# A routed mixture-of-experts layer behind a recurrent attention: out-projection and ranks by tiles of 128 tokens

## The chip, the cores and the metric

The kernel runs on one core of a Trainium2 chip. The metric is the device time of one execution in microseconds (us), a median over several executions. Five engines work side by side, each through its own queue of instructions: TensorE (PE) multiplies and writes to PSUM, its weight loads are listed apart as PEld; VectorE (DVE), ScalarE (ACT) and GpSimd (POOL) do the elementwise work; SyncE (SP) starts transfers. They wait for each other by semaphores (`wait_ge`, `then_inc`).

## What is computed

1088 tokens (16 images or texts with 68 positions each), width 256, everything in float32. The reference, cut to what matters:

```python
h = concat(patches(x) @ W.T + b, (weight_l @ weight_r)[x_txt])        # embed: 36 + 32 tokens each
h = h + attn(layernorm(h))                                             # 16 heads of 64, gated recurrence
h = h + ffn(layernorm(h))                                              # 8 experts, the best 2 of each token
# attn: S_t = a_t * S_(t-1) + k_t v_t^T;  o_t = q_t S_t;  out @ W_o
# ffn:
probs = softmax(xn @ Wg);  top_vals, top_idx = top_k(probs, 2);  top_vals /= sum(top_vals)
out   = sum over the two experts e of top_vals * (relu(xn @ W1[e] + b1[e]) @ W2[e] + b2[e])
```

## The kernel before

It has four stages, each written by hand for every engine, in the order in which the instructions stand in each queue; nothing reorders them.

**Attention** goes by pairs of heads (`HP` = 8 pairs), tokens along the free axis. A pair's scores (L549) and mixes with the values (L565) go by four groups of 272 tokens (`GT`), 12 and 16 matmul instructions each in the trace; between a group's scores and its mix stands the causal mask on DVE (L1168, `mask`). ACT copies each mix into `oT` (L936). Within the pairs 1 to 7 the groups of the pair before stand between the projections of the next pair. The last pair has no next pair beside it: L631 to L635 order its groups as scores 0, scores 1, mix 0, scores 2, mix 1, scores 3, mix 2, mix 3, with two pairs of PSUM banks for the scores. Before it a one-element matmul (L630) and `ok_sum` decide whether a general path is needed (it is not, with these inputs); `s_way` says so to every engine.

**Out-projection, norm, routing.** `out_projection(g, m)` (L672) puts the features on partitions: per group of 272 tokens and half `m` of the width, 8 matmuls with `wo` as weights. DVE adds the result to the stream `hT` (L1263). Mean and variance are matmuls with a matrix of 1/256 (L682, L689), the square and the root are ACT's (L1045, L1049), centring and normalising DVE's (L1269, L1275, L1278). `logits` (L699) has the experts on partitions; ACT copies it (L1053), and `turn_logits` (L749) turns it to tokens on partitions. `turn_stream` (L741) and `turn_rows` (L732) turn the stream and the normalised rows, ACT copies them to `hrow` (L1023) and `xrow` (L1016), SP writes `xrow` to memory (L396, L398).

Only then, for all nine row tiles at once, DVE does the softmax, the two best experts (`top`, `topi`), `pick` (one-hot, 9 tiles x 2 picks x 8 experts) and `share`. Two matmuls (L827 with a strict triangle `tri`, L829 with `mean_w`) count the picks before each token; DVE works out from them the rank of each pick in its expert's blocks of 128 rows (L1334 to L1354), then `in_block` (L1355) and `at_place` (L1359); POOL makes `entry` (L1546). 18 matmuls (L837) turn these into the table of the 24 blocks; DVE takes the row numbers `gather_u` and `scatter_u` out of it. PE runs `keep_warm` in the waits: 7 multiplications of 512 columns before the table, 5 behind it (L484, two instructions each in the trace).

**Experts.** 24 blocks of 128 rows: POOL gathers the rows (L1552), PE turns them (L760), `up` (L777 to L779), `turn_h` (L788), `down` (L798); DVE and ACT copy between; POOL scatters (L1559). w1 is split by POOL into `w1hi` and `w1lo` beforehand (L1537, L1539), once the attention is done and its last quarter has been loaded (L389, L1535).

**Combine.** SP loads both rows of each token, DVE adds them with `share` to `hrow` (L1429, L1433), SP stores.

## Time and profile before

| | us |
|---|---|
| median of 3 runs | 389.0 |
| lowest and highest of them | 388.13, 389.59 |
| the profiled execution, its own time | 388.07 |
| its span, first to last instruction | 386.3 |
| around the span | 1.8 |
| mean granted TensorE clock, as a share of full speed | 0.958 |

The times below are us from the start of the span. The stage of experts begins at 273.4 and its matmuls end at 366.9; the scatter, the loads and the combine take the rest. PE is busy 90% of the span. A float32 matmul shows as two instructions in the trace, one of type float32r as one; a transpose as one.

### The profile page before, as it was taken

To read this page: it belongs to the slowest core of one execution; us is meant where nothing else is said; L and a number is where in the kernel's file an instruction comes from. 1 tells how busy PE (TensorE), PEld (TensorE's weight loads), DVE (VectorE), ACT (ScalarE), POOL (GpSimd) and SP (SyncE) were. 2 spreads that over 40 slices of the span, in tenths; PEclk is the share of its full clock that TensorE was granted. 3 is DMA by queue.
4 is the path that set the end of the run, shared out by engine and by line. 5 is a ranking of instruction groups with operands and counts; after the bars stand their busy time and mean duration, and the time that the engine had idled before them with its cause. 6 is when DMAs were issued, how large, how long until landed. Compare 5 with 4: busy or idle time off the path is not lost.

```text
span 386.3 us, 7120 instructions
## 1 busy us (share of the span) xinstructions
PE 348.6 (90%) x2545; PEld 297.7 (77%) x2546; DVE 219.0 (57%) x333; ACT 115.2 (30%) x255; POOL 139.3 (36%) x147
## 2 busy tenths in 40 slices
PE   4989999999999999999799999698799999999900
PEld 3664999999999999999787886474588888888800
DVE  1056898758586857796930354585344545454326
ACT  1035453353435252523211111530123233232300
POOL 5632025231224113131233995005435555463310
PEclk9999999999999999999989999887999999999965
DMA  7920006022020200000009600030111221222156
GB/s 216 291 86 0 2 5 216 1 88 93 3 97 0 97 2 2 2 2 0 3 2 372 283 0 0 2 116 14 54 42 68 70 75 67 74 71 55 42 171 216
DMA packets 12093, 28.95 MB, mean 75 GB/s; under 512 B 2144, under 2 KB 6752, under 8 KB 11552
## 3 DMA queue, kind: packets, MB, share of 16 engines
q1 hardware_dynamic: 9632, 21.99, 16.0%
q0 software_dynamic: 2432, 6.56, 5.8%
q8 instruction: 20, 0.33, 0.4%
q14 instruction: 9, 0.07, 0.1%
HBM read 23.17 MB, written 5.37 MB: 74 GB/s over the span
## 4 chain that ended last, share of the span: by engine, by line
PE 66%; issue 9%; POOL 8%; DVE 7%; DMA 6%; SPq 1%; ACT 1%; POOLq 0%; DVEq 0%
PE ps L798 10%; PE ps L428 7%; PE ps L549 7%; PE ps L565 6%; PE ps L429 6%; PE ps L430 6%; POOL w1lo L1539 5%; PE ps L777 3%; PE ps L779 3%; PE ps L778 3%; PE ps L525 3%; PE ps L788 3%; DMA pt<-patches 2%; POOL w1hi L1537 2%; PE ps L526 2%
## 5 line engine op out<-in xcount | busy, mean ns | idle before, releaser
L428 PE MATMUL ps<-xnhi,wlo 128*128 128x272 f32 x192 | 57.9, 301 | 0.9 <-DVE xnlo L1136 0.9
L1161 DVE RECIPROCAL invU<-U 128x272 f32<-128x272 f32 x32 | 57.6, 1827 | 0.0
L429 PE MATMUL ps<-xnlo,whi 128*128 128x272 f32 x192 | 55.4, 288 | 0.0
L430 PE MATMUL ps<-xnhi,whi 128*128 128x272 f32 x192 | 55.3, 288 | 0.0
L1037 ACT ACTIVATE hr<-ps,b 128x128 f32<-128x128 f32 x96 | 27.4, 369 | 80.3 <-PE ps L788 80.3
L1486 POOL TENSOR_TENSOR qA<-qraw,invU 128x544 f32<-128x544 f32 x16 | 22.4, 1398 | 71.8 <-DVE invU L1161 34.9
L798 PE MATMUL ps<-w,hr 128*128 x192 | 45.2, 379 | 0.0
L1559 POOL DMA_INDIRECT yrows<-yb,scatter_u x24 | 24.5, 1020 | 40.4 <-DVE yb L1401 36.9
L428 PEld LDWEIGHTS ps<-xnhi,wlo 128*128 128x128 f32 x192 | 36.1, 188 | 2.8 <-issue 1.7
L798 PEld LDWEIGHTS ps<-w,hr 128*128 128x128 f32 x192 | 34.7, 190 | 3.8
L1168 DVE TENSOR_TENSOR pb<-ps,causal 128x592 uint32<-128x592 uint32 (+3 forms) x32 | 27.5, 858 | 17.4 <-PE ps L549 17.1
L429 PEld LDWEIGHTS ps<-xnlo,whi 128*128 128x128 f32 x192 | 36.2, 189 | 0.0
L430 PEld LDWEIGHTS ps<-xnhi,whi 128*128 128x128 f32 x192 | 36.1, 188 | 0.0
L1475 POOL TENSOR_TENSOR wlo<-wraw,whi 128x768 fp32r<-128x768 f32 x8 | 17.5, 2182 | 42.0 <-ACT bneg L897 42.0
L549 PE MATMUL ps<-qA,kU 64*128 64x136 f32 (+8 forms) x384 | 30.8, 294 | 0.7 <-issue 0.7
L565 PE MATMUL ps<-pb,vt 128*64 128x136 f32 (+8 forms) x512 | 29.2, 255 | 2.4 <-DVE pb L1168 2.1
L672 PE MATMUL ps<-oT,wo 128*128 128x272 f32 x128 | 30.5, 394 | 0.7 <-ACT oT L936 0.7
L565 PEld LDWEIGHTS ps<-pb,vt 128*64 128x64 f32 x512 | 25.4, 139 | 7.1 <-DVE pb L1168 3.3
L1552 POOL DMA_INDIRECT xg<-xrows,gather_u x24 | 24.9, 1037 | 14.9 <-issue 6.4
L1143 DVE TENSOR_TENSOR_SCAN U<-u_g,first 128x544 f32<-128x544 f32 x16 | 21.0, 1310 | 16.2 <-ACT u_g L918 16.2
L549 PEld LDWEIGHTS ps<-qA,kU 64*128 64x128 f32 x384 | 27.2, 193 | 3.1 <-issue 0.9
L672 PEld LDWEIGHTS ps<-oT,wo 128*128 128x128 f32 x128 | 24.2, 190 | 6.1 <-issue 1.2
(176 smaller groups left out, 608.2 us busy)
## 6 DMA issues: line engine op xcount, KB each, us to landing
w<-w SPq DMA_DIRECT2D x1, 4096.0 KB, 14.7
wraw<-w_attn SPq DMA_DIRECT2D x8, 384.5 KB, 3.6
w<-w SPq DMA_DIRECT2D x6, 512.0 KB, 4.2
yin<-yrows SPq DMA_DIRECT2D x4, 384.0 KB, 4.7
wv<-w_v SPq DMA_DIRECT2D x4, 256.0 KB, 2.7
wo<-w_o SPq DMA_DIRECT2D x1, 1024.0 KB, 13.4
w<-w SPq DMA_DIRECT2D x1, 1024.0 KB, 5.2
b<-b SPq DMA_DIRECT2D x1, 1024.0 KB, 16.7
```

The lines of the kernel that those rows point to most:

```text
L428: pe.matmul(dst, slo, mhi[n], start=(i == 0), stop=False)
L429: pe.matmul(dst, shi, mlo[n], start=False, stop=False)
L430: last = pe.matmul(dst, shi, mhi[n], start=False, stop=(i == len(pairs) - 1))
L549: last = pe.matmul(ps[:, bank + h, at:at + t1 - t0], kU[par][k, r * P:(r + 1) * P], qA[par][k, t0:t1], start=True, stop=True)
L565: last = pe.matmul(ps[DK * h:DK * (h + 1), bank, lo - GT * g:hi - GT * g], vt[(a // 2) % 2][:, r, par * P + DK * h:par * P + DK * (h + 1)] ...
L672: last = pe.matmul(ps[:, 2 * (g % 2) + m, 0:GT], wo[:, a, m * P:(m + 1) * P], oT[:, a, g * GT:(g + 1) * GT], start=(a == 0), stop=(a == HP ...
L798: last = pe.matmul(ps[:, 5 + par, 0:D], hr[par][:, j * P:(j + 1) * P], w2[:, bass.ds(e, 1), j * D:(j + 1) * D].rearrange("p o n -> p (o n) ...
L1037: last = act.activation(hr[par][:, j * P:(j + 1) * P], ps[:, 3 + par, j * P:(j + 1) * P], ACT.Relu, bias=col)
L1161: dve.reciprocal(invU[:, g * GT:(g + 1) * GT], U[:, g * GT:(g + 1) * GT]).then_inc(s_a, 1)
L1168: dve.tensor_tensor(pb[g % 2][:, :, 0:PW[g]].bitcast(U32), ps[:, bank:bank + 2, 0:PW[g]].bitcast(U32), keep, ALU.bitwise_and).then_inc(s_p, 1)
L1552: pool.indirect_dma_start(out=xg[b % XG][:], out_offset=None, in_=xrows, in_offset=bass.IndirectOffsetOnAxis(ap=gather_u[:, b:b + 1], axis=0),
L1559: pool.indirect_dma_start(out=yrows, out_offset=bass.IndirectOffsetOnAxis(ap=scatter_u[:, b:b + 1], axis=0), in_=yb[b % NY][:], in_offset= ...
```

## The change

The scores of the last pair keep one pair of banks (4 and 5) like those of the other pairs, and its groups run as scores 0, mix 0, scores 1, mix 1, and so on. The out-projection behind them goes by nine tiles of 128 tokens (the last one overlaps the one before by 64), tokens on partitions, with `oT` as weights and `wo` streaming; the stream is added on PE, by two matmuls of `hT` with the identity. ACT copies each tile to `hrow`. DVE takes mean and variance with `bn_stats` and `bn_aggr`, normalises into `xrow`; PE turns each tile (`turn`), ACT copies it (`xT`), PE multiplies it with `wg` (tokens on partitions at once), DVE chooses the two best by `max` and `max_index` of the logits (`choose`), and PE adds each tile's picks into the ranks of all later picks (`count`, in float32r). All of that stands between the tiles of the out-projection. The softmax is taken of the eight sorted logits, behind the table (`low`, `weigh` after the third block). `entry` is made by DVE, pick by pick, beside `at_place`. SP writes each normalised tile twice, once per pick, so `gather_u` comes straight out of the table. POOL's split of w1 no longer waits for the last quarter of w1.

```diff
@@ PE
-                if early(a, HP) and a == HP - 1 and g:
-                    pe.wait_ge(s_p, 4 * a + g - 1)
-                    pe.wait_ge(s_o, 4 * a)
-                    pe.wait_ge(s_vev, VC * IT)
-                elif not (early(a, 1) and g == 0):
+                if not (early(a, 1) and g == 0):
                     pe.wait_ge(s_p, 4 * a + g)
...
-            for g in range(G):
-                pair_scores(HP - 1, 1, g, bank=4 + 2 * (g % 2))
-                if g:
-                    mix(HP - 1, 1, g - 1, bank=3 - (g - 1) % 2)
-            mix(HP - 1, 1, G - 1, bank=3 - (G - 1) % 2)
+            def out_part(r, a0, a1):
+                tok, bank = slice(token0(r), token0(r) + P), OPB[r % len(OPB)]
+                if a0 == 0:
+                    if r >= len(OPB):
+                        pe.wait_ge(s_hrow, r - len(OPB) + 1)
+                    for m in range(DC):
+                        pe.matmul(ps[:, bank, m * P:(m + 1) * P], hT[:, m, tok], ident[:], start=(m == 0), stop=False)
+                for a in range(a0, a1):
+                    last = pe.matmul(ps[:, bank, 0:D], oT[:, a, tok], wo[:, a, :], start=False, stop=(a == HP - 1))
+                if a1 == HP:
+                    last.then_inc(s_op, 1)
+            pair_scores(HP - 1, 1, 0)
+            mix(HP - 1, 1, 0, bank=6)
+            pair_scores(HP - 1, 1, 1)
+            mix(HP - 1, 1, 1, bank=7)
...
+            for r in range(4):
+                out_part(r, 0, HP)
+            out_part(4, 0, half_a)
+            turn(0)
+            out_part(4, half_a, HP)
+            turn(1)
+            out_part(5, 0, half_a)
+            logits(0)
...
+            out_part(8, half_a, HP)
+            logits(5)
+            turn(6)
+            count(5)
+            turn(7)
+            logits(6)
+            pe.wait_ge(s_hrow, 6)
+            keep_warm(1, 0)
+            turn(8)
+            count(6)
+            logits(7)
+            logits(8)
+            count(7)
+            count(8)
...
-            keep_warm(7, 3)
+            keep_warm(3, 0)
             for a in range(A):
-                if a % RT == 0:
-                    pe.wait_ge(s_place, a // RT + 1)
-                    pe.wait_ge(s_entry, a // RT + 1)
+                pe.wait_ge(s_place, a + 1)
@@ DVE
+            def take_moments(r):
+                dve.wait_ge(s_hrow, r + 1)
+                link(dve.bn_stats(spread[r % 2][:], hrow[:, r]))
+                dve.bn_aggr(moments[:, r], spread[r % 2][:]).then_inc(s_mom, 1)
+            def choose(r):
+                dve.wait_ge(s_lgmm, r + 1)
+                logits = ps[:, 6, r * E:(r + 1) * E]
+                link(dve.max(top[:, r, :], logits))
+                link(dve.max_index(topi[:, r, :], top[:, r, :], logits))
+                dve.tensor_tensor(pick[:, r], expert_no[:, r],
...
+            for r in (7, 8):
+                take_moments(r)
+                choose(r - 3)
+                normalise_of(r)
+            for r in range(6, RT):
+                choose(r)
...
-            for i in range(PICKS):
-                a = slice(i * RT, (i + 1) * RT)
-                dve.tensor_tensor(at_place[:, a], place[:].unsqueeze(1).to_broadcast([P, RT, P]),
-                                  place_of[:, a].unsqueeze(2).to_broadcast([P, RT, P]), ALU.is_equal
+            for a in range(A):
+                dve.tensor_scalar(entry[:, a, :], block_start[:], border[:, a:a + 1],
+                                  row_no[:, a // PICKS, a % PICKS:a % PICKS + 1], ALU.is_equal, ALU.mult)
+                dve.tensor_scalar(at_place[:, a, :], place[:], place_of[:, a:a + 1], None, ALU.is_equal
                                   ).then_inc(s_place, 1)
@@ POOL
-            pool.wait_ge(s_w1, 16 * EARLY_W + 16)
+            pool.wait_ge(s_w1, 16 * EARLY_W)
             for e in range(E):
+                if e == EARLY_W:
+                    pool.wait_ge(s_w1late, 16)
```

PE's order at the start of the last pair. Before, L549 (scores) of groups 0 and 1, then L565 (mix) of group 0; `pb` is the masked score tile:

```order
L549 MATMUL ps<-qA_100,kU_98 128x136 x2
L549 MATMUL ps<-qA_100,kU_98 128x144 x2
L549 MATMUL ps<-qA_100,kU_98 128x16 x2
L549 MATMUL ps<-qA_100,kU_98 128x136 x2
L549 MATMUL ps<-qA_100,kU_98 128x160 x2
L549 MATMUL ps<-qA_100,kU_98 128x32 x2
L565 MATMUL ps<-pb_103,vt_102 64x136 x2
```

After (L535 is the scores' line there, L551 the mix's):

```order
L535 MATMUL ps<-qA_101,kU_99 128x136 x2
L535 MATMUL ps<-qA_101,kU_99 128x144 x2
L535 MATMUL ps<-qA_101,kU_99 128x16 x2
L551 MATMUL ps<-pb_104,vt_103 64x136 x2
L551 MATMUL ps<-pb_104,vt_103 64x8 x2
L551 MATMUL ps<-pb_104,vt_103 64x136 x2
L551 MATMUL ps<-pb_104,vt_103 64x16 x2
L535 MATMUL ps<-qA_101,kU_99 128x136 x2
```

The scores of group 1 have moved behind the mix of group 0, and so with the later groups.

PE's order from the end of the out-projection to the table, before (L732, L741: rows turned; L827, L829: counts; L484: `keep_warm`; L837: table):

```order
L741 MATMUL ps<-ident,hT 128x128 x8
L732 MATMUL ps<-ident,xc 128x128 x8
L732 MATMUL ps<-ident,xc 32x128 x2
L732 MATMUL ps<-ident,xc 128x128 x8
L732 MATMUL ps<-ident,xc 32x128 x2
L827 MATMUL ps<-pick,tri 128x144
L829 MATMUL ps<-pick,mean_w 128x144
L484 MATMUL ps<-first,mean_w 128x512 x7
L837 MATMUL ps<-entry,at_place 128x24 x18
```

After, from the last half tile of the out-projection (L627) on (L687: logits, L678: `turn`, L697: `count`, L474: `keep_warm`, L817: table):

```order
L627 MATMUL ps<-wo,oT 128x256 x4
L687 MATMUL ps<-wg,xT_127 128x8 x2
L678 MATMUL ps<-ident,xrow 128x128 x2
L697 MATMUL ps<-pick,ones_m 128x64
...
L678 MATMUL ps<-ident,xrow 128x128 x2
L687 MATMUL ps<-wg,xT_126 128x8 x2
L474 MATMUL ps<-first,mean_w 128x512
...
L697 MATMUL ps<-pick,tri 128x16
L474 MATMUL ps<-first,mean_w 128x512 x3
L817 MATMUL ps<-entry,at_place 128x24 x18
```

The long turns and the two counts of all tiles are gone from here; small pieces of the last tiles have taken their place.

## Rows read from the trace of the kernel before

**Rows 1.** Engines by stretch: length, busy (count) PE, PEld, DVE, ACT, POOL, clock, DMA, GB/s.

```profile
203.33:241.47 38.14, 38.14 (x164) 29.99 (x164) 13.24 (x17) 5.34 (x10) 27.58 (x16) 1.00 0.40 166
241.47:256.15 14.68, 11.70 (x65) 9.21 (x65) 9.12 (x43) 7.67 (x14) 0.00 (x0) 0.77 0.01 2
256.15:266.39 10.24, 8.88 (x33) 5.16 (x32) 8.56 (x22) 0.79 (x2) 3.22 (x2) 0.93 0.33 109
273.36:366.00 92.64, 90.69 (x478) 77.66 (x477) 44.60 (x95) 27.44 (x96) 44.29 (x43) 1.00 0.19 61
```

**Rows 2.** Waits from 200 to 290: who <- for whom: us in total, times, longest.

```profile
POOL entry L1546 <- DVE in_block L1355: 24.4, 1, 24.4
POOL w1hi L1537 <- DMA w<-w: 12.4, 1, 12.4
```

**Rows 3.** Timeline of the last pair: start, duration, engine, line, count [idle before <-releaser].

```profile
193.10 1.44 PE L565 MATMUL ps<-pb,vt 128*64 128x136 f32 x16 [1.85 <-DVE pb L1168]
194.59 2.64 PE L549 MATMUL ps<-qA,kU 64*128 64x136 f32 x24
196.18 0.78 DVE L1168 TENSOR_TENSOR pb<-ps,causal 128x592 uint32<-128x592 uint32 x1 [1.34 <-PE ps L549]
...
199.66 0.99 PE L549 MATMUL ps<-qA,kU 64*128 64x136 f32 x12
...
200.70 0.97 DVE L1168 TENSOR_TENSOR pb<-ps,causal 128x784 uint32<-128x784 uint32 x1 [0.83 <-PE ps L549]
...
201.73 0.92 PE L565 MATMUL ps<-pb,vt 128*64 128x136 f32 x16 [0.24 <-DVE pb L1168]
...
203.33 11.24 PE L672 MATMUL ps<-oT,wo 128*128 128x272 f32 x48 [0.68 <-ACT oT L936]
```

**Rows 4.** PE alone by stretch: length, busy (count), granted clock, DMA, GB/s.

```profile
191.00:192.00 1.00, 0.24 (x6) 1.00 0.00 0
192.00:193.00 1.00, 0.00 (x0) 1.00 0.00 0
...
194.00:195.00 1.00, 1.00 (x14) 0.50 0.00 0
...
197.00:198.00 1.00, 1.00 (x24) 1.00 0.00 0
```

**Rows 5.** Back-to-back small PE work; the first is from the chain, the rest timeline.

```profile
281.96 1.73 PE ps L798 x8
...
241.47 1.07 PEld L741 LDWEIGHTS ps<-ident,hT 128*128 128x128 f32 x10 [0.46 <-issue]
...
249.03 1.03 PEld L749 LDWEIGHTS ps<-ident,lgT 8*128 8x128 f32 x9 [1.29 <-issue]
...
262.96 1.08 PEld L837 LDWEIGHTS ps<-entry,at_place 128*128 128x128 f32 x9 [1.67 <-DVE at_place L1359]
```

**Rows 6.** DVE and ACT pieces: timeline rows, and lines by source (ns min/median/max).

```profile
251.87 0.71 DVE L1312 MAX8 top<-pr 128x8 f32<-128x8 f32 x9
256.15 0.31 DVE L1334 TENSOR_SCALAR total<-ps 128x144 f32<-128x144 f32 x1 [0.95 <-PE ps L829]
260.35 0.18 DVE L1354 TENSOR_TENSOR border<-pos,place_of 128x18 f32<-128x18 f32 x1
375.06 1.28 DVE L1429 SCALAR_TENSOR_TENSOR yin<-yin,share,hrow 128x256 f32<-128x256 f32 x3 [7.67 <-DMA yin<-yrows]
...
L1195 DVE TENSOR_SCALAR causal<-causal x1: 872/872/872, 45.8 to 45.8; 128x1376 int32<-128x1376 f32 x1
L1366 DVE TENSOR_SCALAR owner_i<-owner x1: 178/178/178, 265.1 to 265.1; 128x24 int32<-128x24 f32 x1
L1026 ACT ACTIVATE hrow<-ps x1: 377/377/377, 243.7 to 243.7; 128x256 f32<-128x256 f32 x1
```

**Rows 7.** Timeline of PE at the table and behind it.

```profile
264.62 1.73 PE L837 MATMUL ps<-entry,at_place 128*128 128x24 f32 x9 [0.48 <-POOL entry L1546]
266.20 7.32 PE L484 MATMUL ps<-first,mean_w 128*128 128x512 f32 x10
```

More of the change, by code:

```diff
@@ L744, in turn_logits @@
-            def turn_logits():
-                pe.wait_ge(s_lgt, G)
-                for r in range(RT):
-                    t0 = min(r * P, TOK - P)
-                    last = pe.transpose(ps[:, 4, r * E:(r + 1) * E], lgT[:, t0:t0 + P], ident[0:E, 0:E])
-                last.then_inc(s_lgtok, 1)
+            turn(3)
+            out_part(6, 0, half_a)
+            logits(2)
+            count(0)
+            out_part(6, half_a, HP)
+            logits(3)
+            count(1)
+            turn(4)
@@ new lines, in _ @@
+            out_part(7, 0, half_a)
+            count(2)
+            out_part(7, half_a, HP)
+            count(3)
+            logits(4)
+            turn(5)
+            out_part(8, 0, half_a)
+            count(4)
+            out_part(8, half_a, HP)
[10 more added lines that the diff above has]
+            logits(8)
@@ L1071, in _ @@
-            stream_rows(1, 5, RT)
-            rows(2, 0, 6, 3)
-            rows(3, 1, 0, 2)
+            act.activation(pr[:], low[:], ACT.Exp).then_inc(s_exps, 1)
             act.wait_ge(s_owner, 1)
@@ new lines, in _ @@
+            normalise_of(4)
+            choose(0)
+            take_moments(5)
+            choose(1)
+            normalise_of(5)
+            choose(2)
+            take_moments(6)
+            choose(3)
+            normalise_of(6)
+            for r in (7, 8):
[4 more added lines that the diff above has]
+                choose(r)
+            rank = ps[:, 7, 0:A * E].rearrange("p (a e) -> p a e", e=E)
@@ L1418, in _ @@
                 block_step(b, b % 2)
+                if b == 2:
+                    weigh()
             copy_h(NB - 1, 1)
```

428 lines of the change are left out of this document (164 added, 264 removed).

## The prediction

> **What bounds the kernel now.** I read the engines by stretch first, then the timeline around the last pair, then the waits. Up to 203 the kernel is attention and barely touched. From 203.33, the first matmul of the out-projection, to 241.47 PE has no gap [rows 1]: that stretch is PE's own work. From 241.47 to 256.15 PE is busy 11.70 of 14.68 us at a mean clock of 0.77, because norm, logits, softmax and choice hand over to each other. From 256.15 to 266.39 DVE is busy 8.56 of 10.24 us: it works out ranks and table while PE fills the time with `keep_warm`. Then the ten `keep_warm` instructions behind the table run, 7.32 us to the end of the last [rows 7], and the experts start at 273.36. Their stretch has PE busy 90.69 of 92.64 us and is not touched, nor is what follows. So the time of the change is the time from 194.59, the first scores of the last pair [rows 3], to 273.36: 78.8 us, of which 8.7 lie before 203.33 and 70.0 behind it.
>
> POOL looks prominent in the chain of waits with its split of w1, but it then waits 24.4 us for DVE's `in_block` [rows 2]. Taking the last quarter of w1 out of its first wait, part of the 12.4 us there, moves work with over 20 us of cover. I count nothing. The cover stays, since the table comes no earlier than some 60 us after the attention's end. Writing the normalised rows twice is covered too: 18 transfers, issued between PE's tiles, the last about 10 us before the gather that needs it; SP has nothing else to do there.
>
> **The last pair: a loss, and the largest term.** Before, PE has the next group's scores to do while DVE masks. After, it has nothing: scores g+1 stand behind mix g, and mix g waits for mask g. At full clock a group's scores take about 0.95 us (0.99 with the end of the last) and a mix 0.80 (0.92 with its end) [rows 3]. The four masks grow from 0.78 to 0.97 us, together 3.5. With 0.2 us per group for handing over (scores end to mask about 0.05, mask end 201.67 to mix 201.73 and up to 0.15 elsewhere) and the 0.68 us to the first out-projection, the pair takes 4 x 1.75 + 3.5 + 0.8 + 0.7 = 12.0 us against 8.74: 3.3 more.
>
> That holds at full clock. The trace shows what gaps do just there: PE is idle from 191.24 to 193.10, and then the clock is at 0.50, 1.2 GHz, through 194 to 196, and back at 2.4 GHz by 197 after PE had worked without a gap [rows 4]. At the low level the mix of 16 took 1.44 us and the first scores lasted from 194.59 to the mask at 196.18, about 1.5 us [rows 3], so a group costs 1.5 + 1.37 instead of 1.75, 1.12 more. The kernel after enters the pair in the same state, but then works about two thirds of the time with a hole of about 1 us in each group, where before it had none. I expect that not to bring the clock back, or to bring it back and lose it again: three of four groups at the low level, 3.4 more. Term: **+6.7**.
>
> The out-projection then starts at 1.2 GHz. The shortest low stretch in the trace lasts 3.4 us, from 193.3 to 196.6, its inside in [rows 4]; half speed over it loses 1.7 us. Term: **+1.7**.
>
> A rule speaks to this. In the Trainium skill, page "TensorE: Matmul & The Clock Gate", section "Why this matters for your kernels", only idle gaps between bursts that are clearly longer than these are said to throttle the engine. By it the pair would cost the 3.3 us alone, and the sum would be the first rival's below. This case's trace does not bear it out: the clock fell behind a gap of 1.85 us.
>
> **From the first tile to the last: PE work.** Nearest row for a float32 matmul with 256 streaming columns is L798: 8 instructions in 1.73 us, 0.216 each [rows 5]. A tile has 8 of them, 16 instructions: 3.46 us. The addition of `hT` is 4 instructions of 128 columns; the turns of L741 pass at 1.07/10 = 0.107 [rows 5] and I take that, 0.43 a tile. The upper end is the 0.19 that one weight load lasts, if those are not hidden: 3 us more over nine tiles. Nine tiles: 35.0. Between them, up to the last tile's end: six turns (12 x 0.107 = 1.3), five logits (20 instructions; L749 with 8 columns passes at 0.115: 2.3), five counts (16 instructions; L837 with 24 columns passes at 0.12: 1.9). I add 0.9 for some thirty switches between short runs, an estimate at 0.03 each. Together **41.4**, where before 38.1 went to 241.47: 1152 instead of 1088 tokens and the additions on PE cost what mean and variance gave back. DVE and ACT keep up here: per tile of over 4 us DVE has under 2 us.
>
> **From the last tile to the ranks.** Here steps wait for each other. Counted from tile 8's end: the copy on ACT 0.1 + 0.38 (L1026); `bn_stats` of 256 about 0.42 and `bn_aggr` 0.2, with a handover 0.7; `choose(5)`, which DVE has in front of `normalise_of(8)`, three small instructions of 0.18 with two handovers, 0.67; reciprocal and normalisation 0.65. That is 2.5. PE meanwhile does count 5, turn 7, logits 6 and stands at 3.0; `keep_warm(1)`, two instructions of 0.43, delays turn 8 to 3.9. Then turn 8, count 6, logits 7, which `choose(7)` follows, logits 8, `choose(8)`, count 8: 0.25 + 0.36 + 0.5 + 0.65 + 0.5 + 0.7 + 0.4. The ranks stand 7.4 us behind the last tile. Most of PE's pieces here are tiny, so I give 0.4 for the low clock in `keep_warm`, which costs 0.85 if it falls wholly there: **7.8**. Before, from 241.47 to the start of L1334 at 256.15 [rows 6], the same took 14.7. This is where the change gains.
>
> **Ranks to table.** Before, L1334 at 256.15 to the end of L1354 at 260.53, 4.4 us in 15 instructions [rows 6]; ten of them are left, at their durations 2.7, with the wait 2.8: **2.8**. Then `in_block`, `at_place` and POOL's `entry` took 5.8 us up to 266.35, the end of the table [rows 7]. After, DVE does 36 small instructions. Bounds: L1366 lasts 0.178 with 24 elements, but small instructions without a wait between them start closer together, nine MAX8 in 0.71 us, 0.08 each. `at_place` has 128 elements; `tensor_scalar` did 1376 in 0.87 us, so 128 are about 0.23. Operands per partition cost more: L1429 lasts 0.48 where 256 elements without one last 0.43, and three of them take 1.28, so 0.08 of each overlaps [rows 6]. A pair is at least 0.08 + 0.15, at most 0.18 + 0.29 (no overlap, no fast mode). By L1429, the row nearest in form, 0.155 + 0.20 = 0.355: 18 x 0.355 = **6.4**, between 4.1 and 8.5. PE's matmul behind the last: **0.3**. The three `owner` instructions, 1.3 us, now stand in DVE's queue ahead of `gather_u`; the gathers then land about 6.5 us after the table, just inside the `keep_warm` that follows it.
>
> The Trainium skill, page "VectorE: DVE Perf Modes", section "The TRN2 errata — SBUF-src ops pay a fixed extra latency per instruction", speaks against cutting work this small: every instruction pays its fixed latency. With all of it paid, by L1366 and the 0.23 above, a pair is 0.41 and the loop 7.3 instead of 6.4. The MAX8 row shows that part of it overlaps.
>
> **Behind the table.** `keep_warm(5)` is the same; it ran at the low level first, since PE had done little during the table, and so it will again: **7.0** from 266.35 to 273.36. Its ten instructions at full clock would be 4.3, at the low one 8.5.
>
> **Sum.** Behind the last pair: 41.4 + 7.8 + 2.8 + 6.4 + 0.3 + 7.0 = 65.7 against 70.0, so -4.3. With +6.7 and +1.7: **+4.1**. `weigh`, 1.4 us on DVE after the third block, lies beside PE's work in a stage where DVE is busy 44.60 of 92.64 us: nothing, at worst 1. The profiled execution would be 388.1 + 4.1 = 392.2. It lay 0.9 below the median of the runs; on the median 389.0 the same difference gives 393.1, which I forecast.
>
> **Rivals.**
> *The clock holds in the last pair* (or comes back after the first scores as before). For it: from 197 on the clock was full before, with gaps of 0.24 and 0.68 us at the pair's end [rows 3]. Against: a hole in every group. Then +3.3, +0.6 for the first scores at the low level, no half-speed start, -4.3: 388.6. Chance 0.26.
> *The tail is shorter than I think, with the clock held.* The decision lies in the loop: at 0.23 a pair it is 4.1 us instead of 6.4, and with `keep_warm` ending at the full level 1 us more is won. Then about 385.5. It beats the loss in the last pair from the point at which everything from the first tile to the experts takes under 64 us. Chance 0.16.
> *Everything low.* All four groups at 1.2 GHz (+1.1), a second low stretch at the out-projection (+1.7), slow loads for the additions (up to +3): 397. Chance 0.10.
> *The routing isn't hidden*: PE stalls between tiles for `choose` or the copies, several tenths in each, as each logits waits for the choice before. DVE has 2 us of slack per tile, so small: within the forecast's width.
>
> **How the numbers follow.** Forecast 0.48, 390.5 to 395.5. Range for 8 in 10: from 386.0, which cuts off most of the second rival, to 396.5. A change within 0.5% (1.9 us) cannot be told from none in this kernel. Slower by more: forecast and third rival, 0.56. Within: the first rival and the forecast's lower edge, 0.27. Faster by more: 0.17.
>
> **What would show it.** In the trace after: PE's groups in the last pair at 2.7 us each (clock held) or 3.9 (low), and the clock in the first microseconds of the out-projection; 41.4 us from first to last tile; 7.8 from there to the first rank instruction; the spacing of the 36 small instructions. The forecast is wrong above all if the clock is at 1.00 through the last pair, or if the steps behind the last tile take much more or less than 8 us.

## The result, and the profile after

The changed kernel took 393.58 us (median of 4 runs, 392.58 to 395.94), the kernel before beside it 388.56 us (388.01 to 389.59): a ratio of 1.0145, with a 95% interval of 1.0094 to 1.0196. It is slower. Medians in this document are over all runs, while the ratios and their intervals leave out a run that lies over 1.5% above the fastest of its kernel (none here; in the series below four of f1, two of e3 and one of the kernel before in each). The forecast was 393.1, on the same side and inside its range; three of its steps came out about 1 us too low each, which smaller ones and luck partly made up for.

The profiled execution took 393.43 us, 5.4 more than the one of before (388.07), so the sum of the prediction (+4.1) can be laid beside it term by term. First the engines by stretch in the kernel after. The columns are those of [rows 1]: window and length, busy time (count) of PE, PEld, DVE, ACT and POOL, granted clock, DMA share, GB/s.

```profile
194.35:210.93 16.58, 12.03 (x114) 11.10 (x113) 3.64 (x5) 1.99 (x5) 2.35 (x17) 0.54 0.01 2
210.93:216.04 5.11, 5.11 (x14) 4.30 (x15) 0.00 (x0) 1.49 (x2) 4.94 (x4) 0.50 0.83 309
210.93:254.61 43.68, 43.25 (x231) 38.54 (x231) 17.90 (x52) 8.43 (x24) 26.81 (x16) 0.94 0.50 193
254.61:262.51 7.90, 5.86 (x37) 4.94 (x37) 3.36 (x21) 3.31 (x7) 0.00 (x0) 0.87 0.07 17
262.51:265.12 2.61, 2.61 (x4) 1.06 (x5) 2.26 (x11) 0.00 (x0) 0.00 (x0) 0.50 0.00 0
265.12:272.37 7.25, 6.39 (x21) 4.00 (x19) 7.25 (x37) 0.00 (x0) 0.00 (x0) 0.74 0.00 0
272.37:279.43 7.06, 7.05 (x13) 3.12 (x13) 1.67 (x10) 0.26 (x1) 3.13 (x3) 0.64 0.19 56
```

The windows are, in this order: the last pair; the first 5.11 us of the out-projection, which are part of the next window; all nine tiles; from the last tile to the first instruction of the ranks; the ranks; VectorE's loop over 18 columns; and from there to the first turn of gathered rows. The last pair took 8.74 us before and takes 16.58. From its end to the first turn the kernel before took 70.0 us [rows 1, 3] and this one takes 68.5. So the out-projection and ranks did become shorter, by 1.5 us, and the pair became longer by 7.8. In the loop's window DVE is busy for all of it.

The timeline of PE in the pair (start, duration, engine, line, operation, names, shape, count, and in brackets the idle time before it and what ended that) answers to [rows 3]. L535 are the scores, L551 the mix, L625 the first instruction of the out-projection:

```profile
193.39 0.92 PE L551 MATMUL ps<-pb,vt 128*64 128x136 f32 x16 [1.85 <-DVE pb L1140]
...
194.35 0.88 PE L535 MATMUL ps<-qA,kU 64*128 64x136 f32 x12
196.11 1.52 PE L551 MATMUL ps<-pb,vt 128*64 128x136 f32 x16 [0.88 <-DVE pb L1140]
197.56 1.63 PE L535 MATMUL ps<-qA,kU 64*128 64x136 f32 x12
...
208.69 1.60 PE L551 MATMUL ps<-pb,vt 128*64 128x136 f32 x16 [1.08 <-DVE pb L1140]
210.93 1.19 PE L625 MATMUL ps<-ident,hT 128*128 128x128 f32 x4 [0.65 <-ACT oT L916]
```

Each mix waits 0.88 to 1.08 us for DVE's mask. Before, the next scores hid this wait, except for 0.24 us at the last mix. And everything from the first mix on takes almost twice its time: 1.52 where the first mix of a pair could be 0.88, 1.63 where the scores could be 0.92. The reason is the clock. PE by stretch, with its busy time (count), the granted clock, DMA share and GB/s:

```profile
191.00:194.00 3.00, 1.15 (x22) 1.00 0.00 0
194.00:195.00 1.00, 1.00 (x22) 1.00 0.00 0
195.00:196.00 1.00, 0.23 (x6) 0.78 0.00 0
196.00:197.00 1.00, 0.89 (x10) 0.50 0.00 0
...
215.00:216.00 1.00, 1.00 (x4) 0.50 0.91 385
216.00:217.00 1.00, 1.00 (x6) 0.98 1.14 492
```

The clock falls from 2.4 to 1.2 GHz within the microsecond that starts at 195, is 0.50 through the rest of the pair, and comes back just after 216. Before, it fell earlier, at 193.3, and was back by 197 [rows 4].

### The profile page after: what moved, and what is told of

It is laid out like the page before. It is cut to its first block, busy times and chain, and to the rows that moved or that the text cites. A ratio compares the mean times of both kernels' runs of the same rounds, so it can differ in the third digit from the quotient of the medians.

```text
span 391.7 us, 7260 instructions
## 1 busy us (share of the span) xinstructions
PE 351.2 (90%) x2574; PEld 305.3 (78%) x2575; DVE 220.6 (56%) x381; ACT 113.3 (29%) x263; POOL 135.7 (35%) x145
## 4 chain that ended last, share of the span: by engine, by line
PE 78%; DVE 11%; DMA 4%; issue 3%; SPq 1%; ACT 1%; POOL 0%; POOLq 0%; DVEq 0%
PE ps L803 10%; PE ps L627 8%; PE ps L535 7%; PE ps L551 7%; PE ps L418 7%; PE ps L420 6%; PE ps L419 6%; PE ps L782 3%; PE ps L784 3%; PE ps L783 3%; PE ps L515 3%; PE ps L793 3%; DMA pt<-patches 2%; PE ps L516 2%; PE ps L517 2%
## 5 line engine op out<-in xcount | busy, mean ns | idle before, releaser
L1496 POOL DMA_INDIRECT xg<-xrows,gather_u x24 | 24.9, 1037 | 47.0 <-DVE scatter_u L1310 35.7
L551 PE MATMUL ps<-pb,vt 128*64 128x136 f32 (+8 forms) x512 | 31.3, 267 | 6.0 <-DVE pb L1140 5.8
L551 PEld LDWEIGHTS ps<-pb,vt 128*64 128x64 f32 x512 | 27.4, 147 | 11.0 <-DVE pb L1140 7.4
L627 PE MATMUL ps<-wo,oT 128*128 128x256 f32 x144 | 35.7, 398 | 0.0
L535 PE MATMUL ps<-qA,kU 64*128 64x136 f32 (+8 forms) x384 | 32.2, 302 | 0.7 <-issue 0.7
L535 PEld LDWEIGHTS ps<-qA,kU 64*128 64x128 f32 x384 | 28.4, 199 | 3.2 <-issue 1.3
L627 PEld LDWEIGHTS ps<-wo,oT 128*128 128x128 f32 x144 | 27.9, 201 | 3.6
```

Of the source, the lines that this page charges most:

```text
L535: last = pe.matmul(ps[:, bank + h, at:at + t1 - t0], kU[par][k, r * P:(r + 1) * P], qA[par][k, t0:t1], start=True, stop=True)
L551: last = pe.matmul(ps[DK * h:DK * (h + 1), bank, lo - GT * g:hi - GT * g], vt[(a // 2) % 2][:, r, par * P + DK * h:par * P + DK * (h + 1)] ...
L627: last = pe.matmul(ps[:, bank, 0:D], oT[:, a, tok], wo[:, a, :], start=False, stop=(a == HP - 1))
L1496: pool.indirect_dma_start(out=xg[b % XG][:], out_offset=None, in_=xrows, in_offset=bass.IndirectOffsetOnAxis(ap=gather_u[:, b:b + 1], axis=0),
```

## The experiments

All are compared with the kernel before on the same chip: 387.93 us beside e1 to e4 (median of 25 runs), 388.15 beside f1 to f4 (23), 388.13 beside g1 to g4 (11). The three series ran on three chips, and the result apart from them; where kernels of two series are compared, keep in mind that the kernels before beside them differ by up to 0.6 us. Runs of one kernel spread by 2 to 10 us, mostly with the mean clock of the run, so I go by the traces for where time went, and by medians only where they differ by more than that allows.

| kernel | last pair | us, median (range, runs) | ratio to before [95%] |
|---|---|---|---|
| e1 | old order | 386.31 (384.55–388.45, 10) | 0.9959 [0.9917, 1.0002] |
| e2 (old kernel) | new order | 394.79 (392.11–395.96, 4) | 1.0184 [1.0117, 1.0251] |
| e3 | new order, holes filled | 387.21 (384.12–392.04, 10) | 0.9976 [0.9934, 1.0019] |
| e4 | new order, tiles in the holes | 390.37 (387.68–393.31, 10) | 1.0048 [1.0001, 1.0095] |
| f1 | new order, gap ahead filled | 389.07 (385.36–394.78, 10) | 0.9978 [0.9938, 1.0017] |
| f2 | old order, gap ahead filled | 381.85 (380.62–384.37, 6) | 0.9837 [0.9798, 0.9875] |
| f3 | f2, loop as large instructions | 381.26 (378.58–383.11, 6) | 0.9821 [0.9782, 0.9860] |
| f4 (old kernel) | gap ahead filled | 387.34 (385.49–389.42, 10) | 0.9969 [0.9939, 0.9998] |
| g1 | f2, 3 `keep_warm` for 5 | 382.58 (381.29–383.72, 6) | 0.9846 [0.9795, 0.9897] |
| g2 | f3, 3 `keep_warm` for 5 | 379.46 (376.69–381.08, 6) | 0.9771 [0.9714, 0.9828] |
| g3 | g1, none in the tail | 382.14 (380.04–382.92, 6) | 0.9828 [0.9773, 0.9882] |
| g4 | g2, none in the tail | 379.09 (377.68–379.40, 6) | 0.9754 [0.9703, 0.9804] |

My theory after the result: the last pair's new order costs all of the slowdown, by its holes and by the clock that they keep low, and the new out-projection with its ranks is a gain. Rival: the new out-projection itself is the slower one, and the pair only looks so.

### Half of the change alone: e1 and e2

e1 is the changed kernel with the last pair in the old order:

```diff
-            pair_scores(HP - 1, 1, 0)
-            mix(HP - 1, 1, 0, bank=6)
...
+            for g in range(G):
+                pair_scores(HP - 1, 1, g, bank=4 + 2 * (g % 2))
+                if g:
+                    mix(HP - 1, 1, g - 1, bank=3 - (g - 1) % 2)
+            mix(HP - 1, 1, G - 1, bank=3 - (G - 1) % 2)
```

> The kernel after, with one part undone: the last pair's scores use two pairs of banks again and stand one group ahead of the mixes, as before the change. Theory (the last pair's holes and the low clock that they keep are the whole loss): the pair takes about 8.7 us again instead of 16.6, the out-projection starts at full clock and saves another 2.5, everything behind is as in the kernel after; 393.4 - 7.9 - 2.5 = 383.0, 5 us faster than before the change. Rival (the tiles and ranks cost time themselves): at or above 388.

e2 is the kernel before with only the pair in the new order, the same edit the other way round.

> The kernel before, with only the last pair's groups put in the order scores, mix, scores, mix on one pair of banks. Theory: the pair grows by 7.8 us and the first matmuls of the out-projection run at 1.2 GHz for 3 to 5 us, which costs 1.7 to 2.5; 388.6 + 10 = 398.6. Rival (waits alone, the clock comes back as it did before): plus 3.3 to 3.9, 392.

e1 took 386.31 us, 7.3 below the changed kernel; e2 took 394.79, 6.9 above the kernel before. (The changed kernel was timed apart from them. Each against the kernel before beside it, e1 is at -1.6 and the changed kernel at +5.0, a difference of 6.6.) So the new order costs some 7 us on either kernel, the slowdown is all in it, and the rival is out. Neither size was as expected, though: e1 is 3 us above its forecast, and e2 nearly 4 below its own, between theory and rival. For e1 the timeline of PE and the pair's row by stretch, in the columns of [rows 1], show why:

```profile
193.46 0.92 PE L555 MATMUL ps<-pb,vt 128*64 128x136 f32 x16 [1.83 <-DVE pb L1141]
...
194.43 2.98 PE L539 MATMUL ps<-qA,kU 64*128 64x136 f32 x24
...
203.62 2.06 PE L555 MATMUL ps<-pb,vt 128*64 128x136 f32 x32
206.41 0.68 PE L629 MATMUL ps<-ident,hT 128*128 128x128 f32 x4 [0.72 <-ACT oT L917]
```

```profile
194.43:206.41 11.98, 11.26 (x115) 10.78 (x113) 3.65 (x5) 1.98 (x5) 2.41 (x16) 0.58 0.01 1
```

There is no hole in this pair until its end, and still it takes 12.0 us, at a mean granted clock of 0.58. The 24 scores take 2.98 us, where at full clock they take 1.62 (f2, below). So the clock had fallen behind the gap of 1.83 us ahead of the pair, as in the kernel before, but here it stayed low for some 10 us of work without a pause, where it was back after about 3 in the trace of before. The length of a low stretch is not set by the gap alone, and I had taken the shortest one for the rule.

In e2 the pair grew as expected, but its profiled execution (392.11 us, the lowest of four) got part of it back further on. The first row is the pair, the second the useless products behind the table, which took 7.32 us before [rows 7]:

```profile
194.10:210.03 15.93, 12.02 (x114) 11.09 (x113) 3.64 (x5) 1.59 (x4) 2.06 (x15) 0.55 0.00 1
272.52 4.54 PE L484 MATMUL ps<-first,mean_w 128*128 128x512 f32 x10
```

The pair took 7.2 us more than before, and the out-projection began with 2.7 us at 0.50. The ten useless instructions then ran at full clock, which gave back 2.8 us of the loss. Whether the other three runs, at 394.4 to 396.0, have this too, no trace shows.

### Filling the holes: e3 and e4

e3 puts one useless product of 512 columns into each hole:

```diff
             pair_scores(HP - 1, 1, g)
+            keep_warm(1, 0)
             mix(HP - 1, 1, g, bank=6 + g % 2)
```

> The kernel after, plus one useless product of 512 columns (two instructions, 0.86 us at full clock) between the scores and the mix of each group of the last pair, where PE waits for the mask. It takes no wait away, only the hole. Theory (the clock is what costs most): the clock comes back within the pair as before the change, a group costs about 2.7 us, the out-projection starts at full clock; 386 to 388. Rival (the waits cost, not the clock): 393 or a little more.

It took 387.21 us, as the theory of the clock has it, though three of its ten runs lay at 389.9 to 392.0, with a mean clock of 0.945 to 0.954 for 0.957 to 0.966 in the others. PE in the profiled execution (timeline), and its stretch 194.57 to 206.40 in the columns of [rows 1]:

```profile
193.61 0.92 PE L551 MATMUL ps<-pb,vt 128*64 128x136 f32 x16 [1.85 <-DVE pb L1144]
...
200.84 1.12 PE L474 MATMUL ps<-first,mean_w 128*128 128x512 f32 x2
201.92 0.90 PE L551 MATMUL ps<-pb,vt 128*64 128x136 f32 x16
```

```profile
194.57:206.40 11.83, 11.15 (x123) 7.61 (x121) 3.65 (x5) 1.99 (x5) 2.36 (x17) 1.00 0.01 1
```

With the same gap of 1.85 us ahead of it, the clock is at 1.00 through the whole pair, and the pair takes 11.83 us. That splits the growth of the pair: 11.83 against 8.74 is the part that remains at full clock (3.1 us, the prediction said 3.3), and 16.58 against 11.83 is what the low clock costs in the pair (4.8, the prediction said 3.4). The 8.74 of before holds some low clock itself: at full clock throughout the old order takes 7.90 (f4, below), so the waits of the new order cost 3.9 us and not 3.1. The useless products cost almost nothing there, since DVE's mask takes as long: the groups start 2.7 to 2.8 us apart, where the prediction had 2.7 without them.

e4 puts useful work there, the first seven head pairs of tiles 0 to 3:

```diff
             pair_scores(HP - 1, 1, g)
+            out_part(g, 0, HP - 1)
             mix(HP - 1, 1, g, bank=6 + g % 2)
...
             for r in range(4):
-                out_part(r, 0, HP)
+                out_part(r, HP - 1, HP)
```

> The kernel after, with the first four tiles of the out-projection over the heads of pairs 0 to 6 (18 instructions each, about 3.5 us) between the scores and the mix of each group of the last pair; the rest of each tile behind the pair. The work in the holes is needed anyway. Theory: no holes, full clock, and about 1 us less than with the overlapped order, since no wait for a mask is left: 382. Rival (the mix and its copy now start late and the last one delays the rest): 384 or more.

It took 390.37 us, 3 us more than e3, and my expectation of a gain failed. The clock held in the pair. But what had been moved forward was missing later as a cover. PE's rows with its two longest waits, between the pair and 235:

```profile
224.56 0.41 PE L685 MATMUL ps<-ident,xrow 128*128 128x128 f32 x2 [1.50 <-ACT xT L1026]
231.28 0.58 PE L694 MATMUL ps<-wg,xT 128*128 128x8 f32 x4 [1.79 <-DVE pick L1256]
```

PE stands 1.50 us for the copy of a turned tile and 1.79 for a choice; behind this the clock was at 0.50 from 233.10 to 239.90. This is the last rival of the prediction, the routing that isn't hidden. It was of no weight in the changed kernel, where PE waits once, for 0.43 us, between its first out-projection and 254.61.

DVE is what PE waits for, and DVE is slow here for a reason that the prediction did not have. The same normalisation of 128x256 in e4, twice among the first tiles and once later:

```profile
224.42 2.32 DVE L1249 TENSOR_SCALAR xrow<-hrow,moments,rstd_r 128x256 f32<-128x256 f32 x1
227.86 2.35 DVE L1249 TENSOR_SCALAR xrow<-hrow,moments,rstd_r 128x256 f32<-128x256 f32 x1
243.89 0.41 DVE L1249 TENSOR_SCALAR xrow<-hrow,moments,rstd_r 128x256 f32<-128x256 f32 x1
```

The two long ones lie over POOL's subtractions `w1lo` (224.24 to 226.60 and 227.72 to 230.06) and end 0.14 and 0.15 us after them; from 243.77 on POOL has none and the same instruction takes 0.41. The changed kernel has it too (2.04 us at 222.66, 0.41 from 240.25 on), but with more of PE's work beside it. So in these rows DVE's normalisation ends only when POOL's subtraction has ended. No run without POOL's split was made, so how much of e4's loss that is stays open.

### What brings the clock down: f1, f2, f4

Each of these has two useless products (four instructions) where PE stood idle ahead of the pair:

```diff
+            pe.wait_ge(s_vev, VC * IT)
+            keep_warm(2, 6)
             mix(HP - 2, 0, G - 1)
```

f1 is the changed kernel with them, f2 is e1 with them, f4 the kernel before with them.

> The changed kernel, with two useless products of 512 columns put ahead of the last product of pair 6, so that TensorE works through the 1.85 us in which it stood idle ahead of the last pair. The groups of the last pair are as in the changed kernel, with their holes of some 1 us. Theory A (the idle stretch of 1.85 us brings the clock down, and the holes only keep it there): the clock stays at 1.00 in the last pair, which takes some 12.0 us instead of 16.6, and the time is 386 to 388. Theory B (the holes of some 1 us are enough by themselves to bring the clock down from full): the pair takes 15 to 16.5 us and the time is 392 to 394.

> The changed kernel with the order of the kernel before in the last pair (each group's scores ahead of the mix of the group before it) and the same two useless products ahead of the pair. Without those two, this order took 12.0 us, at 0.50 from just ahead of the pair on. Theory A (the idle stretch ahead of the pair brought the clock down): the clock is at 1.00 through the pair, the pair takes 8.7 us, and the time is some 3 us below the 386.3 of the kernel without the two products, at 383 to 384. Theory B (something within the pair brings it down): as without them, 386 to 387.

> The kernel before, with the two useless products ahead of the last pair, so that TensorE does not stand idle there. Theory A (the clock of the last pair's first scores was already 0.88 to 1.00 in the kernel before, so that nothing is to be had): within 0.5 us of the kernel before. Theory B (the idle stretch sometimes brings the clock down there, and costs some 1 us of the pair): 0.5 to 1.5 us faster.

f2 took 381.85 us, below every run of the kernel before. PE works through the gap, and the pair passes in 7.9 us at full clock. Its timeline and its stretches:

```profile
192.39 1.98 PE L474 MATMUL ps<-first,mean_w 128*128 128x512 f32 x4
194.31 0.92 PE L555 MATMUL ps<-pb,vt 128*64 128x136 f32 x16
...
195.27 1.62 PE L539 MATMUL ps<-qA,kU 64*128 64x136 f32 x24
```

```profile
195.15:203.20 8.05, 6.99 (x118) 6.42 (x115) 3.61 (x5) 1.99 (x5) 2.50 (x17) 1.00 0.01 2
203.20:244.49 41.29, 40.74 (x231) 36.61 (x231) 18.38 (x52) 8.42 (x24) 26.86 (x16) 1.00 0.54 205
244.49:251.94 7.45, 5.11 (x38) 4.19 (x37) 3.36 (x21) 3.31 (x7) 0.00 (x0) 0.98 0.07 18
```

So for the old order theory A holds: the idle stretch ahead of the pair brought the clock down. I had expected 383 to 384; it became 1 to 2 us less, of which 0.8 are explained: the low clock in e1 cost 4.1 us of the pair and not 3.3.

f1 does not decide as neatly. Its profiled execution shows a fall without any idle stretch ahead of the pair:

```profile
191.82 1.98 PE L474 MATMUL ps<-first,mean_w 128*128 128x512 f32 x4
...
196.46 0.88 PE L551 MATMUL ps<-pb,vt 128*64 128x136 f32 x16 [0.88 <-DVE pb L1142]
197.26 0.92 PE L535 MATMUL ps<-qA,kU 64*128 64x136 f32 x12
199.12 1.55 PE L551 MATMUL ps<-pb,vt 128*64 128x136 f32 x16 [0.94 <-DVE pb L1142]
```

```profile
191.87:195.29 3.42, 3.42 (x33) 2.08 (x33) 2.03 (x4) 0.40 (x1) 2.29 (x5) 1.00 0.00 0
195.29:198.70 3.41, 2.01 (x36) 1.77 (x32) 1.25 (x2) 0.40 (x1) 1.68 (x13) 1.00 0.02 5
198.70:209.93 11.23, 8.08 (x73) 7.42 (x73) 2.25 (x3) 1.19 (x3) 0.08 (x1) 0.50 0.01 1
209.93:215.77 5.84, 5.84 (x16) 4.85 (x17) 0.00 (x0) 1.49 (x2) 5.67 (x4) 0.50 0.94 355
```

PE is busy all the time from 191.87 to 195.29, and the clock falls at 198.70. By then PE had had one hole of 0.88 us and stood 0.5 us in the second, which lasted 0.94. So no long gap is needed. But its ten runs do not all look like that. Four took 385.4 to 386.4 us with a mean clock of 0.964 to 0.966, two took 388.5 and 389.7 with 0.953 and 0.954, and four took 392.3 to 394.8 with 0.936 to 0.948; the profiled one is of the last kind. The median of all ten, 389.07, is 0.9 above the kernel before. The first kind has the mean clock of f2 (0.961 to 0.967), and lies near e3. That its clock held through the pair is likely, but only the profiled run has a trace. The changed kernel, with gap and holes, had 0.928 to 0.941 in all four runs. What can be said: the holes of some 1 us in each group can bring the clock down by themselves, and by the mean clocks they do so in some executions and not in others. With the gap in front it was so in all four runs of the changed kernel; four are few to call that a rule.

f4 gained 0.8 us on the kernel before, ratio 0.9969 with an interval from 0.9939 to 0.9998. That is theory B's range, but the interval does not shut out theory A. The traces speak for B: theory A took 0.88 for the clock of the first scores, which is the mean of the whole pair of before, while these scores began at 0.50 [rows 4]. The pair takes 7.90 us in f4, from 194.30 to 202.20, and took 8.74:

```profile
202.20 11.24 PE L674 MATMUL ps<-oT,wo 128*128 128x272 f32 x48 [0.65 <-ACT oT L938]
```

f2 against f4 is the comparison that the change deserves. Both have the old order and a clock of 1.00 in the pair, and they differ by the out-projection, norm and ranks alone: 381.85 against 387.34 us on the same chip, the slowest run of the one below the fastest of the other. Their profiled executions differ by 4.5 (381.89 and 386.37), and their traces place it: the way from the first out-projection to the first turn of gathered rows takes 64.9 us (203.20 to 268.09) against 68.6 (202.20 to 270.78), 3.7 less; the wait for the second part of the combined rows, which varies from run to run (below), is 1.8 shorter in f2; and f2's out-projection starts 1.0 later. So of the 4.5 the traces give 3.7 to the new stages.

### The loop and what hides it: f3, g1 to g4

f3 replaces the 36 instructions of the loop by four:

```diff
-            for a in range(A):
-                dve.tensor_scalar(entry[:, a, :], block_start[:], border[:, a:a + 1], ...
-                dve.tensor_scalar(at_place[:, a, :], place[:], place_of[:, a:a + 1], ...
+            link(dve.tensor_tensor(in_block[:], block_start..., border..., ALU.is_equal))
+            dve.tensor_tensor(entry[:], in_block[:], row_no..., ALU.mult)
+            for i in range(2):
+                a = slice(i * RT, (i + 1) * RT)
+                dve.tensor_tensor(at_place[:, a], place..., place_of..., ALU.is_equal)
```

> The kernel with the old order in the last pair and the two useless products ahead of it, in which also the 36 small instructions of the loop over 18 columns (entry and at_place, 7.25 us in the changed kernel) are 4 large ones: one comparison and one product of 128 x 432 and two comparisons of 128 x 1152. Theory A (VectorE's loop sets when TensorE can form the table, and this sets when the first token rows are turned): the four take some 4 us, the table is there 2 to 3 us sooner after the borders, and the time falls by 1.5 to 2.5 us to some 381. Theory B (the 18 table products on TensorE, or the gather's transfers behind them, set the end): the time stays within 0.5 us.

DVE's timeline: the first pair of the loop's 18 in the changed kernel, and then what f3 has for all 18:

```profile
265.12 0.30 DVE L1296 TENSOR_SCALAR entry<-block_start,border,row_no 128x24 fp32r<-128x24 f32 x1
265.32 0.28 DVE L1298 TENSOR_SCALAR at_place<-place,place_of 128x128 fp32r<-128x128 f32 x1
```

```profile
253.67 0.61 DVE L1299 TENSOR_TENSOR in_block<-block_start,border 128x432 f32<-128x432 f32 x1
254.31 0.61 DVE L1301 TENSOR_TENSOR entry<-in_block,row_no 128x432 fp32r<-128x432 f32 x1
254.83 2.62 DVE L1305 TENSOR_TENSOR at_place<-place,place_of 128x1152 fp32r<-128x1152 f32 x2
```

The small ones start 0.20 us apart, whether they write 24 elements or 128 in a partition: 36 of them are 7.25 us. The large ones take 3.8 for the same result. In the traces f3 is 2.6 us shorter from the borders to the first turn (11.1 for 13.8), but the medians of f3 and f2 differ by 0.6, and their runs overlap. With five products behind the table the point stayed open, so the last four kernels cross two changes, all with three products behind the table instead of five: large or small instructions, and with or without the useless product in the tail, the `keep_warm(1)` that stands between the last tiles' logits and turns.

> The kernel with the old order in the last pair and the two useless products ahead of it, with 3 instead of 5 useless products behind the table (6 instead of 10 instructions). Theory A (these products and not the first gather set when the first token rows are turned; in the trace of the kernel with five the first gather is issued at 263.6, such a transfer takes 1.0 us to issue and 2.9 to land, so that its rows lie there some 1 to 1.7 us before the turn at 268.1): from the end of the table to the first turn some 4.2 us instead of 5.8, and the time 1 to 1.7 us lower. Theory B (the gather sets it, or the clock falls for it and takes the gain back): within 0.5 us of the kernel with five.

> The same with 3 useless products behind the table, and with entry and at_place as four large instructions. Against the kernel with the 36 small ones and the same 3 products: theory A (VectorE's loop sets when the table is there, and all behind it follows): border to first turn 3 us shorter in the trace, the time 2 to 3 us lower. Theory B (the shorter loop moves work against the clock or the gathers, as the medians 381.3 and 381.9 of the two kernels with five products suggest): within 1 us.

> The kernel with the old order, the filled gap ahead of the pair and 3 products behind the table, without the useless product that stands between the last tiles' logits and turns (2 instructions, 1.10 us). Theory A (it stands on the path from the last tile to the ranks, 0.9 us of which the prediction charged to it): last tile to the first instruction of the ranks 6.5 us instead of 7.45, the time 0.5 to 1 us lower. Theory B (TensorE waits at the picks for as long as it saves, or the clock falls earlier and takes it back): within 0.3 us or slower.

> All of it together: old order in the last pair, gap ahead of it filled, 3 products behind the table, four large instructions for entry and at_place, no useless product among the last tiles. If the parts add up (1.5 for the products behind the table, 2 to 3 for the loop, 0.5 to 1 for the tail, from 381.9): 377 to 378. If the clock takes back what the shorter stretches give: 379.5 to 381.

Fewer products behind the table (g1) gained nothing: 382.58 against f2's 381.85 in the series before, so the gain of 1 to 1.7 us that theory A had did not come. Their place was taken by the next thing. PE in g1, and in g2:

```profile
264.52 5.26 PE L474 MATMUL ps<-first,mean_w 128*128 128x512 f32 x6
...
270.29 0.44 PE L768 MATMUL ps<-ident,xg 128*128 128x128 f32 x2 [0.29 <-DMA xg<-xrows,gather_u]
```

```profile
258.58 4.52 PE L475 MATMUL ps<-first,mean_w 128*128 128x512 f32 x6
...
263.97 0.44 PE L769 MATMUL ps<-ident,xg 128*128 128x128 f32 x2 [0.66 <-DMA xg<-xrows,gather_u]
```

Now PE waits for the second gather. In g1 it also stayed at 1.2 GHz for longer: the mean clock from 264.24 to 269.62 is 0.52, where f2 had 0.72 in the corresponding stretch, so its six instructions took 5.26 us for 6.16 that ten took in f2.

The loop, though, counts fully: g2 is 3.1 us below g1 and g4 3.05 below g3, with no overlap of runs in either pair (the nearest are g2's 381.08 and g1's 381.29); from the borders to the first turn g2's trace takes 9.4 us and g1's 12.9. So VectorE's loop sets when the table is there and all behind it follows, and in f3 a part of that was hidden or lost by chance of the clock (its runs have a mean clock of 0.958 to 0.970); which of them I can't tell.

The product in the tail counts for nothing that can be measured (g3 0.4 below g1, g4 0.4 below g2, runs overlapping). In g3's trace the way from the last tile to the ranks is even longer than in g1's, 7.98 us for 7.42, with the clock down in it. g4 is the best version that was run: 379.09 us, 2.5% below the kernel before and 3.7% below the changed kernel, which was timed apart from it. It is not the 377 to 378 of parts that add up: of the three parts only the loop's gain came.

## Why the prediction held, point by point

**The bound, and what is not on the path.** Right. The experts take 93.4 us from the first turn to PE's end in both traces (273.36 to 366.81, 279.43 to 372.85), so `weigh` costs nothing. POOL begins with w1 at 210.85 in the changed kernel and its last wait is again a long one for DVE: "POOL xg" waits 35.7 us for `scatter_u`. No wait for w1 moved the path. What the prediction did not have is that POOL's split slows DVE beside it (e4); in the changed kernel that reached PE once, as the wait of 0.43 us, behind a choice whose last instruction took 1.76 us at 236.66 and 0.17 to 0.18 later on.

**The last pair: +6.7 predicted, +7.8 measured.** The order at full clock was right in size (3.3, e3 gives 3.1), though both numbers are taken against 8.74 us, which hold 0.8 of low clock; and the view that the clock would fall was right. What the low clock costs was under-estimated twice. I priced a group at the low level 1.12 us above one at the full level: the groups from the second to the fourth start 4.04 and 4.22 us apart, and e3's 2.72 and 2.79, so 1.3 to 1.4 more each, because the ends of mixes and scores and the handovers stretch as well. And the first group was not spared; only its scores ran at full clock.

**The out-projection's start: +1.7 predicted, +2.6 measured.** The step that failed is "the shortest low stretch in the trace lasts 3.4 us", which I took for the length of the next one. The next one lasted from 195.56 to 216.04, of which 5.11 us lie in the out-projection at half speed, with PE busy without a pause.

The prediction weighed a rule against this. In the Trainium skill, page "TensorE: Matmul & The Clock Gate", section "Why this matters for your kernels", the idle gaps that are named as throttling are clearly longer than the ones here. Taken as a bound, it would have given 388.6. The trace of f1 speaks against it as a safe bound: the clock fell with no gap above 0.94 us in front. In e3 the clock held in the pair although a gap of 1.85 us stood ahead, as the rule has it, but there the holes were filled.

**First tile to last: 41.4 predicted.** 43.68 measured, of which 2.55 are the low clock counted above: 41.1. In e1 and f2, at a clock of 1.00, 41.2 and 41.3. The count of instructions by the durations of [rows 5] was good to 0.3 us, and the cheap price for the additions of `hT` was the right end.

**Last tile to ranks: 7.8 predicted, 7.9 measured,** 7.45 in f2 at a clock of 0.98, which leaves the 0.4 for the clock. But two steps inside were not borne out. The 0.4 was for a low clock in `keep_warm`, and that ran at full clock, 1.10 us at 257.30; the clock fell at 260.4, behind it, so the size was right by luck. And the 0.9 us that I charged to `keep_warm(1)` did not come back when it was taken away (g3, g4).

**Ranks: 2.8 predicted, 2.6 measured.**

**The loop: 6.4 predicted, 7.25 measured.** This is the term with a wrong size. I took 0.355 for a pair by L1429, and it is 0.403. Both instructions have operands per partition and last 0.30 and 0.28 us, longer than the 0.178 and 0.23 of the rows without such operands, and the overlap of some 0.09 takes only part of it back. In the Trainium skill, page "VectorE: DVE Perf Modes", section "The TRN2 errata — SBUF-src ops pay a fixed extra latency per instruction", every instruction pays a fixed latency of its own, and the prediction made 7.3 for the loop of that. The trace has 7.25, though by two errors that cancel: the overlap left out, and the operands' cost. The page's advice against many small instructions agrees with what the loop takes in f3, g2 and g4: 3.8 us instead of 7.25.

**Behind the table: 0.3 and 7.0 predicted, 0.44 and 6.6 measured.** That the gathers land just inside the `keep_warm` was right, and g1 showed what it means: four instructions less, and PE waits for the gather.

**What was missing in the sum.** The changed kernel's end is 0.65 us nearer, because the wait for the second part of the combined rows is 0.41 us instead of 1.06; it was 1.99 in f4 and 0.19 in f2, so this varies. And the pair began 0.24 us earlier. Altogether: +1.1 (pair), +0.9 (start), -0.3 (tiles), +0.1 (tail), -0.2 (ranks), +0.85 (loop), +0.1 (PE), -0.4 (`keep_warm`), -0.65 (end), -0.24 (start of the pair) make +1.3 beside the +4.1, which is the 5.4 of the two profiled executions. The profiled execution was forecast 1.2 us too low (392.2). The forecast of the median came out only 0.5 low because I had added the 0.9 us by which the profiled run of before lay below its median, and the changed kernel's lay 0.15 below its own. That is luck, and so is part of the 1.3: three terms were 2.85 too low together, and the end and start of the trace gave 0.9 back that no term had foreseen.

**The rivals.** The one in which the clock holds was put at 0.26 and 388.6; e3, which makes it hold, has 387.2. It is a real case of this kernel, and f1's runs show how near the two lie to each other. The second rival was wrong in its place: the loop is longer than I took it, not shorter. The third, everything low, came true in part: the pair came out 1.1 us above the forecast's term, as this rival had it, though with longer low groups and not with four of them, and the low clock at the out-projection cost 0.9 more, half of the 1.7 that it added. The additions of `hT` were not slow. And the routing is hidden until tiles are moved forward (e4).

## What to carry to other kernels

An order in which one engine waits for the other costs its holes twice when the matmul clock can fall: here, in the profiled runs, 3.9 us of waits and another 7.3 at 1.2 GHz (4.8 in the pair, 2.55 behind it), so part of it fell on the stage behind the holes. The kernel before had lost 0.8 of this already. Before an interleaving is given up to simplify what stands behind it, try the new stage with the old interleaving, and fill the idle stretch in front of it: the out-projection that came out 1.4% slower here is 1.4% faster than the old one where both have the old interleaving and no idle stretch (f2 against f4, 381.85 and 387.34 us). And where a chain of small VectorE instructions releases TensorE, write it as few large ones, but look at what stands behind it (useless products, gathers) before expecting the gain in the total.

## What the runs showed that I had not expected

- The clock stayed at 1.2 GHz for some 10 us of work without a pause in e1 (24 scores in 2.98 us, the pair in 12.0 at a mean of 0.58), but was back after about 3 us in the trace of before, in the same place with the same work.
- One and the same gap of 1.83 to 1.85 us was followed by a fall in the kernel before, in the changed kernel and in e1, and by none in e3 and e4, whose holes were filled. In the changed kernel the clock was still at 1.00 for the first scores behind it.
- With PE busy ahead of them, a hole of 0.88 us and 0.5 us of the next one were enough for a fall in f1's profiled run, while four of its ten runs have the mean clock and time of a kernel in which it held.
- DVE's normalisation of 128x256 lasted 2.32 and 2.35 us where it lay over a subtraction of POOL's, and 0.41 where POOL had none (e4).
- A `tensor_scalar` with operands per partition lasts 0.28 to 0.30 us on DVE for 24 as for 128 elements in a partition, and such instructions start 0.20 us apart.
